# An interaction network in float32 on one core: layer 0 in six tiles and one pass of hi, hi and lo

## The reference, cut to what matters

```python
e = jnp.stack([tbl_0[ids[:, 0]], ..., tbl_38[ids[:, 38]]], axis=1)      # 1024 x 39 x 16
x0, xk, direct = e, e, []
for idx, (W, b) in enumerate([(w0, b0), (w1, b1), (w2, b2)]):           # w0: 39 x 39 x 128; w1, w2: 39 x 64 x 128
    z = relu(jnp.einsum('bhd,bkd,hks->bsd', x0, xk, W) + b[None, :, None])
    if idx != 2:
        xk = z[:, :64, :]
        direct.append(z[:, 64:, :])
    else:
        direct.append(z)
z = jnp.sum(jnp.concatenate(direct, axis=1), axis=-1)                   # 1024 x 256
h = jnp.concatenate([z, dense_ctx], axis=1)
h = relu(h @ W_top1 + b_top1)
h = relu(h @ W_top2 + b_top2)
y = h @ W_top3                                                          # 1024 x 1
```

## Time and profile before

| | before |
|---|---|
| median of 3 runs | 1333.74 us |
| profiled execution, its own time | 1332.7 us |
| its span (what all views are cut from) | 1330.6 us |
| TensorE busy | 1243.1 us, 93% |
| VectorE busy | 1096.0 us, 82% |
| ScalarE busy | 489.6 us, 37% |
| GpSimd busy | 1098.6 us, 83% |
| mean granted TensorE clock | 0.994 of full speed |
| one step in the middle | 76.07 us |

### The profile page before, as it was taken

One profiled execution on the slowest core, in us unless ns is written; L12 is line 12 of the kernel. 1 busy time (PEld: TensorE's weight loads), 2 busy tenths in 40 slices (PEclk: granted clock), 3 DMA queues, 4 the chain that ended last, 5 costly groups with the idle time before them and its releaser, 6 DMA issues.

```text
span 1330.6 us, 14359 instructions
## 1 busy us (share of the span) xinstructions
PE 1243.1 (93%) x3752; PEld 696.1 (52%) x3752; DVE 1096.0 (82%) x831; ACT 489.6 (37%) x496; POOL 1098.6 (83%) x639
## 2 busy tenths in 40 slices
PE   0378999999999999999999999999999999999899
PEld 0234555555555555555555555555555555555455
DVE  1269898988989898898989898898989889898751
ACT  1034333343433434343433334343343434343333
POOL 6789988898888888898898889888898896556461
PEclk9989999999999999999999999999999999999899
DMA  4771808254280907336180825527190733625000
GB/s 117 277 235 43 317 6 272 85 188 170 67 292 23 318 19 236 124 119 239 42 317 4 280 76 179 180 79 280 21 326 14 242 117 112 242 68 172 0 0 0
DMA packets 81241, 196.24 MB, mean 147 GB/s; under 512 B 23983, under 2 KB 35342, under 8 KB 81193
## 3 DMA queue, kind: packets, MB, share of 16 engines
q1 hardware_dynamic: 70953, 193.14, 41.9%
q0 software_dynamic: 10240, 2.64, 2.1%
...
## 4 chain that ended last, share of the span: by engine, by line
POOL 62%; PE 19%; issue 16%; DVE 2%; ACT 1%; POOLq 0%; DMA 0%; SPq 0%; DVEq 0%
POOL lo L453 37%; POOL emb L443 24%; PE acc L819 16%; DVE prod L716 1%; POOL block_idx L432 1%; ACT hi L585 0%; PE xk L873 0%; PE acc L873 0%; DVE hi L726 0%; PE acc L900 0%; POOLq L452 0%; PE xk L876 0%; PE acc L876 0%; DMA base_sb<-base 0%; PE xk L889 0%
## 5 line engine op out<-in xcount | busy, mean ns | idle before, releaser
L716 DVE TENSOR_TENSOR prod<-x_tiles,xk 128x1024 f32<-128x1024 f32 x640 | 743.7, 1214 | 160.6 <-PE acc L819 122.6
L453 POOL TENSOR_TENSOR lo<-prod,hi 128x1024 fp32r<-128x1024 f32 (+1 forms) x288 | 714.5, 2482 | 132.5 <-ACT hi L585 123.4
L819 PE MATMUL acc<-prod,wfull 128*128 128x512 f32 (+2 forms) x1728 | 813.0, 594 | 0.0
L585 ACT ACTIVATE hi<-prod 128x1024 fp32r<-128x1024 f32 (+1 forms) x320 | 338.7, 1058 | 708.1 <-DVE prod L716 684.7
L819 PEld LDWEIGHTS acc<-prod,wfull 128*128 128x128 f32 (+2 forms) x1728 | 326.6, 190 | 251.4 <-issue 216.6
L443 POOL DMA_INDIRECT emb<-table,block_idx x320 | 355.2, 1110 | 67.0 <-issue 59.7
L819 PE MATMUL acc<-hi,whi 128*128 128x512 f32 (+1 forms) x640 | 315.6, 501 | 25.2 <-issue 20.5
L819 PE MATMUL acc<-lo,whi 128*128 128x512 f32 (+1 forms) x576 | 277.6, 563 | 23.6 <-POOL lo L453 23.5
L819 PE MATMUL acc<-hi,wlo 128*128 128x512 f32 (+2 forms) x640 | 251.4, 401 | 0.0
L716 DVE TENSOR_TENSOR prod<-x_stack,x_tiles 117x1024 f32<-117x1024 f32 (+1 forms) x112 | 202.9, 1876 | 28.8 <-DMA x_tiles<-x_rows 28.4
L819 PEld LDWEIGHTS acc<-lo,whi 128*128 128x128 f32 (+1 forms) x576 | 106.4, 190 | 162.4 <-issue 104.9
...
## 6 DMA issues: line engine op xcount, KB each, us to landing
...
```

The source lines that it names most:

```text
L453: nc.gpsimd.tensor_tensor(lo[0:r, product_slot(j), :], prod[0:r, product_slot(j), :], hi[0:r, part_slot(j), :].bitcast(f32), ALU.subtract) ...
L585: nc.scalar.activation(hi[0:r, part_slot(j), :], prod[0:r, product_slot(j), :], ACT.Copy).then_inc(hi_ready, 1)
L716: nc.vector.tensor_tensor(prod[0:r, product_slot(j), :], in0, in1, ALU.mult).then_inc(product_ready, 1)
L819: mm = nc.tensor.matmul(z[:, c], w[0:r], part[0:r, c], start=first and i == 0, stop=last and i == len(weights) - 1)
```

## The change

Layer 0's 780 pairs are laid out anew. The operand has two versions, `x0_stacks`, each with the 39 fields three times (turned by 0, 9 and 24) and 11 more rows (from field 22 or 33 on), so that a product can have 128 rows. Six products with 128, 128, 128, 123, 117 and 117 rows hold 741 pairs. The last 39 pairs are the product of two x0 tiles, of the new kind **T**: its 117 rows hold the same 39 pairs three times. ScalarE rounds all of them; VectorE then subtracts on 39 of the rows (64 to 102), so that `hi` holds hi, hi and lo; and TensorE makes one fast pass with the weights `w_triple`, which are wlo on the first 39 rows and whi on the others.

The kinds of layer 0 are now `GFFTGFF`. It still has seven products, of which two are G as before, four instead of five are F, and one is T. Six x0 tiles instead of seven have two slots (`TA = 6`), fourteen instead of thirteen have one; the order of the shifts changes (`TURNS`). The stacks are loaded by eight DMAs instead of three. A step now has 21 tiles that are not F.

```diff
 PAIRS = (FIELDS + 1) // 2
-SHIFTS = FIELDS // 2 + 1
-PER = 3
-T0 = -(-SHIFTS // PER)
+GROUPS0 = (0, 9, 24)
+TAILS = (22, 33)
+PER = len(GROUPS0)
...
 ROWS0 = PER * FIELDS
-LAST0 = (SHIFTS - PER * (T0 - 1)) * FIELDS
+ENDS = 128 - ROWS0
 REPEATS = 5
 SROWS = REPEATS * FIELDS
 STEP = 2 * T1 + T0
-REST = T1 - T0
-SHIFT = [11 * t % FIELDS for t in range(T1)]
+TA = 6
+REST = T1 - TA
 TWIN = T1 - 1
+TURNS = [0, 1, 4, 5, 7, 9]
+TURNS += [t for t in range(T1) if t not in TURNS]
+SHIFT = [11 * t % FIELDS for t in TURNS]
 assert sorted((SHIFT[t] + 25 * half) % FIELDS for t in range(T1) for half in range(2)) == sorted([0] + [*range(FIELDS)])
 TOP1, TOP2 = 512, 256
...
 
-KINDS = ["GFFGFFF", "GFFGF" * 2 + "GFHGF" + "GFFGF", "GFFGF" + "GFFGF" + "GFHGF" + "GFFGF"]
+KINDS = ["GFFTGFF", "GFFGF" * 2 + "GFHGF" + "GFFGF", "GFFGF" + "GFFGF" + "GFHGF" + "GFFGF"]
 SHORT = 12
-TILES = [list(range(T0)),
-         list(range(T0)) + list(range(T0, T0 + 5)) + [TWIN] + list(range(T0 + 5, TWIN)),
-         list(range(T0, T1)) + list(range(T0))]
+TILES = [[0, 1, 2, 1, 3, 4, 5],
+         list(range(SHORT)) + [TWIN] + list(range(SHORT, TWIN)),
+         list(range(TA, TA + SHORT)) + [TWIN] + list(range(TA + SHORT, TWIN)) + list(range(TA))]
+STACK = [0, 1, 0, None, 1, 0, 0]
+TRIPLE, BESIDE = 3, 2
+ROWS = [128, 128, 128, ROWS0, ROWS0 + 6, ROWS0, ROWS0]
+LO_AT = NEXT
+assert KINDS[0][TRIPLE] == "T" and KINDS[0].count("T") == 1
 assert all(ts[SHORT] == TWIN for ts in TILES[1:])
 assert all(k.count("H") == 1 and k[SHORT] == "H" for k in KINDS[1:])
-SPLITS = [[t for t, k in enumerate(ks) if k != "F"] for ks in KINDS]
+SPLITS = [[t for t, k in enumerate(ks) if k not in "FT"] for ks in KINDS]
 FULLS = [[t for t, k in enumerate(ks) if k == "F"] for ks in KINDS]
 SPLIT_AT = [0, len(SPLITS[0]), len(SPLITS[0]) + len(SPLITS[1])]
+W0_ORDER = SPLITS[0] + FULLS[0] + [TRIPLE]
 FULL_AT = [0, len(FULLS[0]), len(FULLS[0]) + len(FULLS[1])]
...
 def rows(l, t):
     if l == 0:
-        return ROWS0 if t < T0 - 1 else LAST0
+        return ROWS[t]
     return 128
+
+
+def fields0(t):
+
+    p = [*range(128)]
+    if t == TRIPLE:
+        first = [(q + SHIFT[BESIDE]) % FIELDS for q in p]
+    else:
+        first = [(q % FIELDS + GROUPS0[q // FIELDS]) % FIELDS if q < ROWS0 else (q - ROWS0 + TAILS[STACK[t]]) % FIELDS
+                 for q in p]
+    return first, [(q + SHIFT[TILES[0][t]]) % FIELDS for q in p]
+
+
+assert sorted(tuple(sorted(pair)) for t in range(T0) for pair in
+              list(zip(*fields0(t)))[:FIELDS if t == TRIPLE else ROWS[t]]) \
+    == [(h, k) for h in range(FIELDS) for k in range(h, FIELDS)]
+assert fields0(0)[0][:FIELDS] == fields0(0)[1][:FIELDS]
 
...
 
 def tile_slot(parity, tile):
-    return parity * T0 + tile if tile < T0 else T0 + tile
+    return parity * TA + tile if tile < TA else TA + tile
 
 
...
         x0T = sb("x0T", [128, GROUPS, 128])
         stack_at = nc.sbuf_base
-        x0_stack = sb("x0_stack", [128, COLS])
-        SLOTS = 2 * T0 + REST
+        x0_stacks = sb("x0_stacks", [128, len(TAILS), COLS])
+        SLOTS = 2 * TA + REST
...
         wlo = sb("wlo", [128, N_SPLIT, LAYER], f32r)
+        w_triple = sb("w_triple", [128, LAYER], f32r)
         bias = sb("bias", [LAYER, 3])
         wt3_sb = sb("wt3_sb", [128, TOP2 // 128])
...
-                    sp.dma_start(x0_stack[g * FIELDS:(g + 1) * FIELDS, :], rows_ap(m, g, [[COLS, FIELDS], [1, COLS]])
+                for i, tail in enumerate(TAILS):
+                    for g, first in enumerate(GROUPS0):
+                        sp.dma_start(x0_stacks[g * FIELDS:(g + 1) * FIELDS, i, :],
+                                     rows_ap(m, first, [[COLS, FIELDS], [1, COLS]])).then_inc(stack_loaded, 16)
+                    sp.dma_start(x0_stacks[ROWS0:128, i, :], rows_ap(m, tail, [[COLS, ENDS], [1, COLS]])
                                  ).then_inc(stack_loaded, 16)
 
...
             load_stack(1)
-            for tile in range(T0):
+            for tile in range(TA):
                 load_tile(1, 1, tile)
 
...
-                        if not is_step(n, PROLOGUE) or SPLITS[0].index(ORDER[j][1]) >= PARTS:
-
-                            act.wait_ge(tile_used, reached(n, parts_before(n, j), "FDGH"))
+                        act.wait_ge(product_ready, reached(n, j, "FDGHT"))
+                        if not is_step(n, PROLOGUE) or sum(k != "F" for k in KIND[L0:j]) >= PARTS:
+
+                            act.wait_ge(tile_used, reached(n, parts_before(n, j), "FDGHT"))
...
+                if l == 0:
+                    nc.scalar.activation(w_triple[:, :], w0x_stage, ACT.Copy)
...
+            nc.vector.tensor_tensor(wfull[:, 0:f, :], w0f_stage, w0t_stage[:, n:n + f, :], ALU.add)
+            nc.vector.tensor_tensor(w0x_stage, w0x_stage, w0t_stage[:, n + f, :], ALU.add)
+            nc.vector.tensor_tensor(w_stage[:, 0:n, :], w_stage[:, 0:n, :], w0t_stage[:, 0:n, :], ALU.add
+                                    ).then_inc(w0_summed, 1)
...
+                if l == 0:
+                    nc.vector.tensor_tensor(w_triple[0:FIELDS, :], w0x_stage[0:FIELDS, :],
+                                            w_triple[0:FIELDS, :].bitcast(f32), ALU.subtract)
...
                 tile = x0_tiles[0:r, tile_slot(1 - parity if l == 0 else parity, TILES[l][t]), :]
-                in0, in1 = (x0_stack[0:r, :], tile) if l == 0 else (tile, xk[l - 1][0:r, :])
+                if l:
+                    in0, in1 = tile, xk[l - 1][0:r, :]
+                else:
+                    beside = x0_tiles[0:r, tile_slot(1 - parity, TILES[0][BESIDE]), :]
+                    in0, in1 = beside if t == TRIPLE else x0_stacks[0:r, STACK[t], :], tile
                 nc.vector.tensor_tensor(prod[0:r, product_slot(j), :], in0, in1, ALU.mult).then_inc(product_ready, 1)
...
+                if KIND[j] == "T":
+
+                    third = hi[LO_AT:LO_AT + FIELDS, part_slot(j), :]
+                    nc.vector.tensor_tensor(third, prod[LO_AT:LO_AT + FIELDS, product_slot(j), :], third.bitcast(f32),
+                                            ALU.subtract).then_inc(lo_ready_d, 1)
+                    return
...
-                            dve.wait_ge(stack_loaded, PER * 16 * (n + 2))
+                            dve.wait_ge(stack_loaded, len(TAILS) * (PER + 1) * 16 * (n + 2))
...
-                    if j - DELAY >= start and KIND[j - DELAY] in "DH":
+                    if j - DELAY >= start and KIND[j - DELAY] in "DHT":
                         subtract(n, j - DELAY)
...
                         late = None
-                    if KIND[j] == "F":
+                    if KIND[j] == "T":
+                        pe.wait_ge(lo_ready_d, reached(n, j, "DHT"))
+                        mm = multiply(j, [w_triple], hi[:, part_slot(j), :], False, False)
+                        if late is None:
+                            mm.then_inc(tile_used, 1)
+                        else:
+                            lo_part(late, 2)
+                            late = None
...
                         mm = multiply(j, [wfull[:, w, :]], prod[:, product_slot(j), :], j == start, j == stop - 1)
                         if late is None:
                             mm.then_inc(tile_used, 1)
```

More of the change, by code:

```diff
@@ L204, in build @@
         w0f_stage = stage[:, N_SPLIT:N_SPLIT + len(FULLS[0]), :]
-        w0t_stage = stage[:, N_SPLIT + len(FULLS[0]):N_SPLIT + len(FULLS[0]) + T0, :]
-        pairs_r = nc.alloc_sbuf_tensor_at("pairs_r", [128, 1 + SLOTS, COLS], f32r, offset=stack_at)
-        tiles_r = pairs_r[:, 1:, :]
+        w0x_stage = stage[:, N_SPLIT + len(FULLS[0]), :]
+        w0t_stage = stage[:, N_SPLIT + len(FULLS[0]) + 1:N_SPLIT + len(FULLS[0]) + 1 + T0, :]
+        pairs_r = nc.alloc_sbuf_tensor_at("pairs_r", [128, len(TAILS) + SLOTS, COLS], f32r, offset=stack_at)
+        tiles_r = pairs_r[:, len(TAILS):, :]
         wt1_sb = x0_tiles[:, 0, :].rearrange("p (t n) -> p t n", n=TOP1)
@@ L214, in build @@
         wt1d_sb = x0_tiles[0:DIM, 3, 0:TOP1]
-        wt1_hi, wt1_lo = (pairs_r[:, p, :].rearrange("p (t n) -> p t n", n=TOP1) for p in (5, 6))
-        wt2_hi, wt2_lo = (pairs_r[:, p, :].rearrange("p (t n) -> p t n", n=TOP2) for p in (7, 0))
+        wt1_hi, wt1_lo = (tiles_r[:, p, :].rearrange("p (t n) -> p t n", n=TOP1) for p in (4, 5))
+        wt2_hi, wt2_lo = (pairs_r[:, p, :].rearrange("p (t n) -> p t n", n=TOP2) for p in (0, 1))
         own = tile_slot(LAST % 2, 0)
-        logits_r = [pairs_r[:, 1:3, :], tiles_r[:, own + 4:own + 6, :]]
-        top1, top1_hi, top1_lo = ([place[:, 2 * T0 + 6 * c + p:2 * T0 + 6 * c + p + 2, :]
+        logits_r = [tiles_r[:, 0:2, :], tiles_r[:, own + 4:own + 6, :]]
+        top1, top1_hi, top1_lo = ([place[:, 2 * TA + 6 * c + p:2 * TA + 6 * c + p + 2, :]
                                    .rearrange("p t (m s) -> p (t m) s", s=BANK) for c in range(HALVES)]
@@ L357, in load_stack @@
                 sp.nop(nofuse=True)
-                for g in range(PER):
```

(19 more changed lines are left out.)

47 lines of the change are left out of this document (21 added, 26 removed).

## The result

The change makes the kernel slower: 1348.17 us, the median of 4 runs (1346.26 to 1349.6), against 1333.53 (1332.46 to 1334.18) in the same runs. The ratio is 1.011, interval 1.0092 to 1.0127. The forecast was 1337.6 with a range to 1345: the sign is right, the size isn't, and the time lies outside.

What follows compares the result with a forecast made beforehand. TensorE sets the pace and GpSimd holds it up twice a step. 13 x 0.15 + 1.9 = 3.9 us on 1332.7 gives 1336.6; the median lies 1.0 above, so 1337.6. Range 1333 to 1343, with rivals 1325 to 1345.

Steps and rivals of the forecast that it cites:

- it holds for 13 steps, 2 us: Steps with gathers: each gets 0.15 us longer in sum, 13 x 0.15, about 2 us.
- The wait of 1.6 us that it put at T: Layer 0: TensorE waits about 1.6 us for VectorE's subtraction of T, ahead of the pass with `w_triple`.
- A step at full clock: Whole step with gathers: 76.2 us, where a middle step of the kernel before took 76.07.
- the one at L1+15: Layer 1, tile 15: TensorE waits for GpSimd's lo, which comes 0.84 us late where it had been on time.
- GpSimd's at the border: From layer 2 to layer 1: GpSimd's first lo of layer 1 starts 1.8 us late, waiting for hi.
- GpSimd's lo went ahead of VectorE's last product: End of layer 0: GpSimd's lo of tile 4 and a VectorE product collide; one of them takes over 3 us.
- The wait at the last G tile of layer 1: Layer 1, tile 18: TensorE's wait for GpSimd's lo shrinks to 0.2 us from 0.65.
- the count of 21: Layer 1: 21 users of four `hi` slots make GpSimd late, so the layer gets 0.4 us longer.
- The start: Before the first product: five more DMAs ahead of the first tile cost 1.9 us; bounds 0 and 3.7.
- The last steps: Final steps without gathers: T's wait stands against the tile saved, so nothing changes from 75.0 us a step.
- The first, GpSimd keeping up: Layer 1: gather not blocked or lateness absorbed, a step 0.6 us shorter, 1327.8 us in all; chance 27%.
- The fourth (1353): Layer 0: GpSimd's lo gets ahead of T's subtraction, which takes 3 us; 1.2 a step beyond the forecast; chance 7%.

Runs made afterwards that it cites:

- Experiment 1: Kernel after, with TensorE's wait ahead of the pass with `w_triple` filled by seven fast matmuls of zero weights: 1337.82 us, ratio 1.0034.
- experiments 2 and 4: 2: after, with TensorE's wait at L1+15 filled by four zero-weight matmuls, 1340.02 us. 4: after, with T in hi slot 3, not counted, 1332.2 us.
- experiment 3: Kernel before, with six gathers instead of four in layer 0 and two fewer elsewhere, so TensorE waits longer: 1366.11 us, ratio 1.0239.
- e9_no_third: Kernel after with T in hi slot 3, T's subtraction left out and TensorE waiting for T's hi instead: 1331.41 us, ratio 0.9983 to before.
- the slot, e3_slot: Kernel after, with T in hi slot 3 and the other 20 users counted as before: 1332.2 us, ratio 0.999 to before.
- e6_direct: Kernel after, with T in hi slot 3, its subtraction one product earlier and ScalarE's `direct01` behind the rounding of L0+4: 1359.62 us, ratio 1.0193.

## Why the prediction was wrong

- **The step that failed: "it holds for 13 steps, 2 us".** It priced each of TensorE's waits by its own length, at a fixed clock. The wait of 1.6 us that it put at T (1.80) was taken as a cost of 1.6 and nothing else. It measured 1.80, and the clock fell behind it in eight of 15 steps, 11.4 us in all. The prediction had no term for the clock. Experiment 1 takes all drops away by filling that wait and nothing else; in experiments 2 and 4, where it is 1.6 and 1.46, all and all but one are gone; experiment 3 makes drops in the kernel before, by one longer wait. The kernel before shows one too, that begins in a wait of 4.70 us near its end:

```profile
1258.42 0.76 PE L819 MATMUL acc<-hi,whi 128*128 128x512 f32 x1 [4.70 <-ACT hi L585]
...
1260.27 3.54 PE L819 MATMUL acc<-prod,wfull 128*128 128x512 f32 x4
```

- **A step at full clock: right.** 76.1 against the forecast 76.2. T's wait was 1.80 (1.6), the one at L1+15 1.0 late (0.84), GpSimd's at the border 1.91 (1.8; 1.15 in the step before), and GpSimd's lo went ahead of VectorE's last product, which took 3.29 (over 3). The wait at the last G tile of layer 1 is gone instead of 0.2. So the rest of the walk holds; what it called 0.4 for the count of 21 measured 0.5. The sum's 13 x 0.15, 2.0 us, measured 0.0 without the drops: 0.04 in each of twelve steps, and 0.45 less in the first.
- **The start: mis-sized.** The eight issues on the queue took 3.22 us instead of 1.22, the 2.0 of the forecast. From the tile's issue to the product it was 5.49 instead of 5.17. Another 1.2 came ahead of the stack, from two gathers of 1.38 and 2.03 us where before had 0.94 and 1.32. In the experiments with the same loads the first product starts between 52.5 and 53.7, so that the start's price is 2.8 to 3.9; 1.9 was forecast, and 3.7 its bound.
- **The last steps: "nothing" was wrong**, 1.8 us in two. Without gathers the wait at T isn't made good elsewhere: e9_no_third takes 74.61 in the step that takes 75.7 with the subtraction, so that 1.1 of the wait's 1.8 comes back.
- **The sum.** The profiled execution took 1349.6, 13.0 above the forecast's 1336.6: the drops 11.4, the start 1.8, the last steps 1.8, less the 2.0 of the thirteen.
- **The rivals.** The first, GpSimd keeping up, needed the count of 21 to be harmless; with the slot a step was 75.6, not the 75.5 that it priced, but at the start's cost that is no gain. The fourth (1353) came nearest, for a wrong reason: T's subtraction was never blocked, 1.22 in every step.

What stays open: whether the wait at L1+15 has a share in the drops (no run fills it and keeps T's at 1.8); what keeps the time against which every second step of after has a drop; and how far GpSimd alone sets 75.6. The kernel after was timed in four runs of its own and not beside the experiments, which ran on several chips. The chips of experiments 1 and 2 do show drops, in e3_slot and e6_direct.
